# Graph attention's steps: target one-hots copied to two bytes by ScalarE before they are transposed, and the edge values spread by GpSimd in four operations a step

## The reference

```python
h = (x_flat @ W_gat).reshape(M, HEADS, NUM_EXPERTS)          # 4 heads x 4 values
a_src = (h * att_src).sum(-1)
a_dst = (h * att_dst).sum(-1)
e = leaky_relu(a_src[src] + a_dst[dst], negative_slope=0.2)
ee = exp(e - segment_max(e, dst)[dst])
denom = segment_sum(ee, dst)
agg = segment_sum(h[src] * (ee / denom[dst])[:, :, None], dst)
scores = layernorm(agg + b_gat).reshape(M, HEADS, NUM_EXPERTS).mean(1)
# the two largest scores of a node pick and weigh its experts
```

## Time and profile before

| what | value |
|---|---|
| device time, median of 3 runs | 1036.79 us (1032.73 to 1036.92) |
| device time of the profiled execution | 1033.07 us |
| its span from first to last instruction | 1031.2 us |
| busy: TensorE, VectorE, ScalarE, GpSimd | 916.1, 647.2, 367.4, 225.8 us |
| the twelve steps (first transposes to the end of the last sums) | 392.1 to 462.8 us |

### The profile page before, as it was taken

The page is one execution under the profiler, slowest core; times in us unless marked ns, Lnnn a source line. Parts: engine busy times, 40 slices in busy tenths (PEclk is TensorE's granted clock), DMA queues, the critical chain, the costliest instruction groups (busy, mean ns, idle before and its releaser), DMA issues. The chain is left out here.

```text
span 1031.2 us, 17228 instructions
## 1 busy us (share of the span) xinstructions
PE 916.1 (89%) x6731; PEld 460.8 (45%) x6731; DVE 647.2 (63%) x1731; ACT 367.4 (36%) x644; POOL 225.8 (22%) x286
## 2 busy tenths in 40 slices
PE   1897788888999888998898989999999889979998
PEld 0587556653223335773455333333333334443333
DVE  4958566576676447996567554554653656677665
ACT  0112533324544243224435414444445023352232
POOL 2700112123433313430230220121223502200000
PEclk9878989899999998999998988999999989999999
DMA  9300200000000001000000000000000000000000
GB/s 305 91 1 2 84 17 2 2 2 2 0 1 1 1 2 43 1 2 2 1 1 1 1 1 1 1 1 1 1 1 1 1 1 1 1 2 0 6 6 11
DMA packets 11476, 15.40 MB, mean 15 GB/s; under 512 B 8268, under 2 KB 9324, under 8 KB 10398
## 3 DMA queue, kind: packets, MB, share of 16 engines
q1 hardware_dynamic: 9976, 13.20, 4.1%
q10 hardware_dynamic: 1418, 1.09, 0.4%
HBM read 13.76 MB, written 0.52 MB: 14 GB/s over the span
## 5 line engine op out<-in xcount | busy, mean ns | idle before, releaser
L633 DVE TENSOR_REDUCE mx<-PS 128x2 f32<-128x1024 f32 (+3 forms) x104 | 109.7, 1095 | 97.7 <-PE PS L440 94.0
L593 ACT ACTIVATE arena<-PS 128x1024 f32<-128x1024 f32 (+3 forms) x104 | 91.1, 924 | 127.8 <-PE PS L470 127.8
L1231 DVE TENSOR_TENSOR arena<-arena,PS 128x512 f32<-128x512 f32 (+1 forms) x144 | 97.0, 684 | 45.8 <-ACT arena L1206 41.0
L1132 PE MATMUL PS<-XT,late 64*128 64x512 f32 (+1 forms) x288 | 100.6, 640 | 4.8 <-DVE L L1874 2.0
L485 PE MATMUL PS<-arena 128*64 128x512 f32 (+3 forms) x416 | 100.4, 572 | 0.5 <-DVE arena L694 0.4
L465 PE MATMUL PS<-arena 32*128 32x512 f32 (+4 forms) x416 | 76.7, 607 | 10.2 <-ACT arena L570 7.4
L1206 ACT ACTIVATE arena<-PS,f_b_sb 128x512 f32<-128x512 f32 x96 | 61.9, 686 | 64.1 <-PE PS L1132 62.7
L1164 PE MATMUL PS<-arena,late 128*64 128x512 f32 (+1 forms) x288 | 81.6, 617 | 1.0 <-DVE arena L1231 0.7
L440 PE MATMUL PS<-arena 32*128 32x512 f32 (+4 forms) x416 | 69.0, 603 | 4.3 <-ACT arena L566 1.6
L1132 PEld LDWEIGHTS PS<-XT,late 64*128 64x128 f32 (+1 forms) x288 | 28.0, 182 | 55.8 <-ACT arena L1206 41.5
L1206 ACT ACTIVATE arena<-PS 114x512 f32<-114x512 f32 x48 | 27.4, 596 | 67.6 <-PE PS L1134 66.9
(11 more groups left out here) (427 smaller groups left out, 1677.9 us busy)
## 6 DMA issues: line engine op xcount, KB each, us to landing
arena<-in_rel SPq DMA_DIRECT2D x4, 1024.0 KB, 12.0
late<-in_edges SPq DMA_DIRECT2D x2, 1024.0 KB, 11.4
late<-in_w_f_w SPq DMA_DIRECT2D x3, 342.0 KB
arena<-in_adj SPq DMA_DIRECT2D x1, 1024.0 KB, 6.9
late<-in_w_f_w SPq DMA_DIRECT2D x2, 512.0 KB, 3.9
Cc<-in_consts SPq DMA_DIRECT2D x1, 916.0 KB
arena<-in_ids ACTq DMA_DIRECT2D x1, 800.0 KB
late<-in_w_f_w SPq DMA_DIRECT2D x4, 128.0 KB, 3.4
```

What stands on the lines that cost most here:

```text
L593: nc.scalar.activation(PT[:, s % 2, p, :, queries(c)], PS[:, a:a + 2, queries(c)], ACT.Exp, scale=scale).then_inc(exp_done.sem, 1)
L633: v.reduce_max(mx[:, g % 2, c, 2 * p:2 * p + 2], PS[:, a:a + 2, keys(c)], axis=AX.X).then_inc(max_done.sem, 1)
L1132: ins = nc.tensor.matmul(PS[0:rows, up_bank(n), :], w1(i)[r], XT2[r, b * S:(b + 1) * S], start=True, stop=True)
L1231: nc.vector.tensor_tensor(HG[0:rows, n % 4, :], ha, PS[0:rows, gate_bank(n), :], ALU.mult).then_inc(gated_done.sem, 1)
```

## The change

Two edits, both in the twelve steps. First, ScalarE copies the target one-hots of a step to a new 2-byte tile `sOHdh` (`target_hots`) once VectorE has made them, and TensorE transposes that tile as 2-byte data with the 2-byte identity; `turns` waits for the new count `hots_cast` ahead of these four transposes. `sOHd` itself stays, and `sums` still reads it. Second, GpSimd's operation of 1280 elements becomes four of 320, each of which counts up `edges_spread`, and `sums` waits for each piece by itself.

```diff
+    sOHdh = part(1280, [2, C4, P // 2]).bitcast(BF16)
+    hots_cast = Signal(ctx, nc, "step_target_hots_in_two_bytes")
@@ turns(t), TensorE
+                eng.wait_ge(hots_cast.sem, t + 1)
                 for c in range(C4):
-                    ins = nc.tensor.transpose(PS[:, 6, c * P:(c + 1) * P], sOHd[:, t % 4, c], ident)
+                    ins = nc.tensor.transpose(PSh[:, 6, c * P:(c + 1) * P], sOHdh[:, t % 2, c], identh[:])
                 ins.then_inc(hots_turned.sem, 1)
@@ sums(t), TensorE
-                if t < STEPS - 1:
-                    eng.wait_ge(edges_spread.sem, t + 1)
                 for c in range(C4):
                     if t == STEPS - 1:
                         eng.wait_ge(last_spread.sem, c + 1)
+                    else:
+                        eng.wait_ge(edges_spread.sem, C4 * t + c + 1)
@@ GpSimd
-                nc.gpsimd.tensor_tensor(spread[:, t % 2], smasks[:, t % 4, :, 1].unsqueeze(3).to_broadcast([P, C4, 16, SV]),
-                                        vals[:, t % 2].unsqueeze(2).to_broadcast([P, C4, 16, SV]), ALU.mult).then_inc(edges_spread.sem, 1)
+                for c in range(C4):
+                    nc.gpsimd.tensor_tensor(spread[:, t % 2, c], smasks[:, t % 4, c, 1].unsqueeze(2).to_broadcast([P, 16, SV]),
+                                            vals[:, t % 2, c].unsqueeze(1).to_broadcast([P, 16, SV]), ALU.mult).then_inc(edges_spread.sem, 1)
@@ ScalarE
+            def target_hots(t):
+                eng.wait_ge(hots_made.sem, t + 1)
+                nc.scalar.copy(sOHdh[:, t % 2], sOHd[:, t % 4]).then_inc(hots_cast.sem, 1)
+
+            target_hots(0)
             for t in range(STEPS):
                 eng.wait_ge(hots_turned.sem, t + 1)
                 nc.scalar.copy(masksT[:, t % 2], PSh[:, 5, C4 * P:(C4 + 1) * P]).then_inc(hots_copied.sem, 1)
                 nc.scalar.copy(OHsT[:, t % 2], PSh[:, 5, 0:C4 * P].rearrange("p (c n) -> p c n", n=P)).then_inc(hots_copied.sem, 1)
-                nc.scalar.copy(OHdT[:, t % 2], PS[:, 6, :].rearrange("p (c n) -> p c n", n=P)).then_inc(hots_copied.sem, 1)
+                nc.scalar.copy(OHdT[:, t % 2], PSh[:, 6, 0:C4 * P].rearrange("p (c n) -> p c n", n=P)).then_inc(hots_copied.sem, 1)
+                if t + 1 < STEPS:
+                    target_hots(t + 1)
                 if t >= 1:
                     eng.wait_ge(scores_made.sem, t)
                     nc.scalar.activation(vals[:, (t - 1) % 2, :, HV:SV], sm[5], ACT.Exp).then_inc(weights_made.sem, 1)
@@ taken(t), VectorE
                 if t >= 2:
-                    eng.wait_ge(edges_spread.sem, t - 1)
+                    eng.wait_ge(edges_spread.sem, C4 * (t - 1))
```

## The result

| | before | after |
|---|---|---|
| device time, median | 1034.76 us (4 runs, 1032.02 to 1036.92) | 1049.29 us (4 runs, 1046.85 to 1054.01) |
| device time and span of the profiled execution | 1033.07 and 1031.2 us | 1046.85 and 1045.1 us |

The changed kernel takes 1.016 times as long (95% interval 1.012 to 1.0199; the two medians by themselves give 1.014). The prediction was 1046 us, 1038 to 1056. Ratios here leave out runs in a slower state, over 1.5% above the fastest of the same kernel (two of before, and four of the twelve in the last row of experiments 9 to 12), while medians and counts of runs have them in.

A forecast was written before the change was run, and what follows sets the result against it. VectorE was taken to set the pace inside the steps, TensorE 0.20 us behind. Terms 7.4 + 0.2 + 2.0 + 0.4 + 1.0 + 0.3 = 11.3 us, on 1035, gave 1046 us, range 1038 to 1056.

The forecast's parts named there:

- The stall behind the copy: In eight passes VectorE's `weighted` waits for ScalarE's exponential, now behind the copy: 0.93 us each, 7.4 us (7.0 to 8.2).
- The pieces: GpSimd's four operations release VectorE's blocked chain later: +0.25 us a pass, 2.0 us in eight (-0.8 to 3.4).
- my working from that rule (+0.1 a pass): By mutual exclusion alone, VectorE's line 2591 (L2602 after) waits for one GpSimd piece at most: near +0.1 us a pass.
- my step from there to +0.43: With no gap between GpSimd's pieces, VectorE may be shut out for all four: line 2591 released 0.43 us later.
- The passes at both ends: Terms outside the eight passes: first pass +0.4, late last values +0.2, end of steps +1.0, start +0.3 us.
- The block that I had put at +0.4: In pass 1 GpSimd's later spread lies over VectorE's line 2591 (L2602 after): +0.4 us (0 to 0.9).
- The +0.2 for late last values: At the last pass TensorE's transposes, waiting for the copy, put off the last values by 0.2 us (0.1 to 0.3).
- At the end of the steps: The last GpSimd spread ends later, over VectorE's scores of the last step: +1.0 us (0.3 to 1.3).
- At the start: The first copy stands behind ScalarE's table load, so the first target transposes begin later: +0.3 us (-0.2 to 1.0).
- The block did not go away: Rival, chance 0.10: gaps between pieces let line 2591 through, -0.84 us a pass, paying for the stall: 1035 to 1039 us.
- Nor was the stall hidden: Rival, chance 0.04: the exponential is done in time and line 2591's release is kept, -6.7 us, about 1028 us.
- TensorE's clock did not fall inside the steps: Rival, chance 0.10: idle TensorE gets the lower clock in half of the eight passes, +14 us, near 1060 us.

The follow-up runs named there:

- experiments 9 to 12: Four kernels side by side: before again, after again, before plus the idle instruction, experiment 8 again; medians 1032.54, 1049.81, 1045.58 and 1033.65 us.
- Experiment 3: The changed kernel with ScalarE's exponential moved ahead of the copy of the next target one-hots; 1045.36 us, ratio 1.0136 to before.
- experiment 1: The changed kernel with GpSimd's spread kept as one operation, so only the copy and 2-byte transposes come; 1047.06 us, ratio 1.0156 to before.
- experiment 2: Before with only GpSimd's spread cut into four operations, and the sums' waits for each; 1038.49 us, ratio 1.0058.
- experiments 4 and 5: Before with GpSimd's spread in two pieces of 640 elements, and in eight of 160; one run each, 1043.92 and 1042.43 us.
- After again: The changed kernel, unaltered, measured once more beside before again; 1049.81 us (6 runs), ratio 1.015.
- before again: The kernel before, unaltered, measured once more as a kernel of its own; 1032.54 us (12 runs), ratio 0.9991 to before.
- the idle instruction: Before plus one VectorE reduce over 1080 constants that nobody reads, between the one-hots and `weighted` in each pass; 1045.58 us, ratio 1.0086.
- experiment 7: Before with 2-byte copy and transposes, one spread, exponential ahead of the copy, target one-hots made first and counted by themselves; 1034.07 us, ratio 0.9996.
- experiment 8: Experiment 7 plus the PSUM operands of experiment 6, against before; 1036.12 us, ratio 1.0009; measured again 1033.65 us, ratio 0.9959.
- experiment 6: Before with the second operands of VectorE's lines 2591 and 2592 read from PSUM; 1037.50 us, ratio 1.0039.

## Why the prediction was right

**The stall behind the copy, 8 x 0.93 = 7.4.** Right in mechanism and within its bounds: 0.89 a pass, 7.1 in the eight, against bounds of 0.87 to 1.03. The copy takes 0.62 us, as its nearest row said (0.627), and the exponential starts 0.09 before its record ends. Experiment 3 takes the stall away by order alone, and experiment 1 has it alone.

**The pieces, 8 x 0.25 = 2.0.** 0.29 a pass, 2.3 in the eight (experiment 2 and the timeline). The pieces start 0.68 us apart, as worked out. What I left open is settled by experiments 4 and 5: VectorE is let in at each boundary, with one instruction. So the pass is lengthened neither by how much later GpSimd ends nor by nothing: 0.14 with two pieces, 0.29 with four, 0.10 with eight. The Trainium skill (SBUF — State Buffer, section Who interferes with whom) has the two engines exclude each other for the whole of an instruction. The trace agrees, L2602 and L2603 being held to the ends of the third and fourth piece; that L2602 waits for one piece at most is right too, and my working from that rule (+0.1 a pass) failed where I took the chain behind L2602 to be free. By the Trainium skill's GPSIMD Engine Reference (section 2.1, Instruction dispatch) a GpSimd core starts the next instruction as soon as it is done with its share of the one before. The trace shows no gap either, for the pieces stay 0.68 us apart; what failed is my step from there to +0.43, since VectorE gets in all the same.

**The passes at both ends.** The sum of the ends came out near what I had, +1.8 against +1.9, by other ways. The block that I had put at +0.4 behind the second `reduce_max` is there: L2602 takes 0.65 at 402.71 us, 0.44 more than the 0.21 that it takes there before. But I counted the stall only in the eight passes of my stretch, and the third `reduce_max` is behind one too: +0.89, forgotten. Against it stand two gains I did not have. The first pass, where VectorE waits for TensorE, is 0.28 shorter; it measures 6.06 to 6.13 us in five profiles with the 2-byte transposes and 6.30 to 6.35 in five without, all at a granted clock of 0.72 or 0.73 there. In the other four that clock was 1.00 and the pass took 4.54 to 5.58 us, so this gain is likely and not shown by itself. And in the last pass VectorE's wait for TensorE, 0.88 us, is gone, because TensorE had been waiting all along and has caught up. I had written that this wait swallows a stall; but that pass makes no one-hots and has none. The +0.2 for late last values is wrong: no wait is left there. At the end of the steps +1.10 against +1.0: L2626 and L2627 take 0.76 us each in place of 0.21, under the pieces that start at 462.00 us. At the start +0.35 against +0.3. After again, one of the four at clock 1.00, splits the same sum another way: +0.78 at the start, -1.04 for the first pass and +1.98 up to the third `reduce_max`.

**The sum** for the stage was 11.3 us and it is 11.27 in the profiles of the first pair, 11.6 in those of the second. That it meets the sum so closely is partly luck: 0.9 forgotten and 1.0 not seen cancel.

**The total.** Medians put the difference at 14.5 us, and at 16 in the second comparison, so some 3 to 5 us lie outside the stage. My forecast of the time, 1046, had none of this and is low by that much. The granted clock is what differs there. The 165 us behind the stage, in before and in after:

```profile
468.00:633.00 165.00, 145.03 (x905) 68.29 (x903) 97.72 (x324) 66.17 (x119) 30.05 (x51) 0.91 0.00 1
```

```profile
475.40:640.40 165.00, 146.25 (x871) 68.94 (x871) 94.60 (x319) 62.60 (x116) 30.02 (x51) 0.86 0.00 1
```

The same stretch in before again, in after again and with the idle instruction:

```profile
464.20:629.20 165.00, 145.09 (x885) 67.64 (x883) 95.70 (x321) 64.42 (x117) 30.03 (x51) 0.89 0.00 1
```

```profile
479.30:644.30 165.00, 145.13 (x885) 67.57 (x883) 95.69 (x320) 64.38 (x117) 30.02 (x51) 0.89 0.00 1
```

```profile
477.90:642.90 165.00, 145.59 (x861) 69.72 (x859) 94.80 (x320) 62.05 (x114) 30.03 (x51) 0.85 0.00 1
```

The figure behind GpSimd's is the granted clock, and it moves between 0.85 and 0.91 in code that no kernel here changes: at 0.86 in after, but at 0.89 in after again, with the part behind the stage 569.7 and 566.8 us long. Ahead of the stage it is alike: where the stage began 3.9 us later in before than in after, the clock in the first 100 us was 0.86 against 0.93, and where it began 3.5 us later in after again than in before again, the clock from 100 to 200 us was 0.88 against 0.93. Fewer instructions get done in the stretch where it is lower (871 matmuls at 0.86, 905 at 0.91). To see what the clock makes in the totals I took 145 runs of before, of after and of the variants in 1 to 3 and 6 to 12, those that the ratios are made of, each with its time and its mean granted clock over the span, and fitted one level for each kernel and one slope for all. The slope is -0.63 us (± 0.05, two standard errors, as below) for 0.001 of clock:

| kernel (runs) | mean clock | mean time over before, us | the same at equal clock, us | stage over before, us |
|---|---|---|---|---|
| before (71) | 0.949 | 0 | 0 | 0 |
| after (10) | 0.943 | +16.2 | +12.5 ± 1.1 | +11.3, +11.6 |
| copy alone (4) | 0.941 | +14.7 | +9.4 ± 1.6 | +8.1 |
| pieces alone (10) | 0.947 | +4.6 | +3.3 ± 1.0 | +0.8 |
| exponential first (4) | 0.938 | +12.4 | +5.2 ± 1.7 | +2.8 |
| operands from PSUM (10) | 0.940 | +4.6 | -1.1 ± 1.1 | -2.1 |
| experiment 7 (10) | 0.948 | +0.5 | -0.5 ± 1.0 | +0.1 |
| experiment 8 (18) | 0.945 | +0.1 | -2.5 ± 0.8 | -3.6 |
| idle instruction (8) | 0.950 | +13.2 | +13.4 ± 1.1 | +9.8 |

At equal clock the change costs 12.5 us, 1 us from its stage; the copy alone and the pieces alone add up to 12.7; and the order of the kernels is nearly that of their stages; the 3.7 us that are left go with a mean clock lower by 0.006. That is a correlation over whole runs. It shows that what lies outside the stage goes with the clock, and it accounts for most of experiment 3, whose stage is 2.8 us longer and whose mean 12.4. It does not show why after's runs got less clock than before's, nor whether they always would: within before alone the clock goes from 0.938 to 0.957 and the time from 1041 to 1028 us. Still, the difference is unlikely to be chance: after's ten runs have a mean clock of 0.943 and before's 71 of 0.949, with a spread of 0.005 (standard deviation) from run to run in either, and experiment 6, with neither copy nor pieces, has 0.940. The idle instruction, with passes as long as after's, has 0.950; so longer passes alone do not bring the lower clock, and a cost of the change by way of the clock, some 3 to 4 us, stands as a rival that no run here tests.

The idle instruction stays 3.6 us above its stage at equal clock, and the pieces alone 2.5. Much of that is in the profiles: in these two the clock was 0.76 and 0.75 from L2224 to the first `reduce_max` and 1.00 from there to the second, against 0.58 and 0.73 in before, and the two pieces took 12.8 and 11.7 us together against 14.4. With before's 14.4 their stages would be some 11.5 and 3.5 us over before (an estimate), against 13.4 and 3.3 at equal clock. What stays open: which stretches of unchanged code lose the clock, and whether the change brings it about.

**The rivals.** The block did not go away: L2602 and L2603 take 0.80 + 0.70 = 1.50 us in a pass, and before they took 1.07 + 0.16 = 1.23. Nor was the stall hidden. TensorE's clock did not fall inside the steps (1.00 in the stretch), though its 1.3 us of idle a pass was there as I had worked out; where the clock was lower was behind the stage or ahead of it, of which the rival did not speak. Of the versions tried, experiment 8 is the one that could beat both kernels: it shortens the stage by 3.6 us, but its ratio was 1.0009 in one comparison and 0.9959 (0.9928 to 0.999) in the other, and there the median of its twelve runs, 1033.65 us, is that of before beside them, 1033.56. Of its 22 runs 9 had a mean clock of 0.938 or less, and took 1039 to 1044 us; of before's 73 runs 7 had. So the shorter stage is shown, and a gain in the total is not.

## What to carry to other kernels

Work moved to an idle engine costs by its place in that engine's list: 0.62 us of ScalarE cost 0.89 a pass ahead of an instruction that others wait for, and nothing behind it with its input made first. Shrinking a transpose pays only where its engine sets the pace: the 2-byte transposes gained nothing in experiment 7 and 0.16 us a pass in experiment 8. So find that engine by the waits, not by busy time. Where GpSimd runs beside a VectorE chain with two SBUF operands, putting one of VectorE's operands in PSUM shortened the pass by 0.27 us, and cutting GpSimd's operation lengthened it by 0.10 to 0.29; but no median here shows the program faster for it.

## What the runs showed of the hardware

- Beside back-to-back GpSimd operations, VectorE's two-SBUF-operand instructions go one at each boundary, and GpSimd's next piece starts on time (0.68 us apart for 320 elements, 0.41 for 160). The chain then moves at GpSimd's beat: with eight pieces five such instructions of 0.16 to 0.22 us end 0.37 to 0.41 us apart.
- With one operand in PSUM the same instruction takes 0.22 us under a GpSimd operation, not 1.07.
- Each further GpSimd operation costs 0.14 us: 2.34, 2.48, 2.76 and 3.33 us for one, two, four and eight (the last near 0.14 x 7 = 1.0 over the first).
- A change of 0.001 in the mean granted clock went with 0.63 us of the program's time, between kernels and within one, so two medians of one kernel can differ by some 4 us: before's were 1036.79 (3 runs) and 1032.47 (13).
